# Fewer unread products in the prologue of a fused attention and MLP block, and one row tile moved from GpSimd to ScalarE

## The reference

```python
mod = (_silu(L0_c) @ L0_wmod).reshape(8, 6, 1, -1)
sa, ca, ga, sb, cb, gb = (mod[:, k] for k in range(6))
ga, gb = sign(ga) * max(|ga|, 0.25), sign(gb) * max(|gb|, 0.25)
h = _layernorm(x) * (1 + ca) + sa
scores = einsum('nsd,ntd->nst', h * w_lhs, h * w_rhs)
x = x + ga * einsum('nst,ntd->nsd', softmax(scores, axis=2), h)
h = _layernorm(x) * (1 + cb) + sb
x = x + gb * (relu(h @ W1 + b1) @ W2 + b2)
```

## Time and profile before

| | us |
|---|---|
| median of 3 runs | 678.64 |
| lowest and highest of them | 678.5, 679.3 |
| the profiled execution | 679.18 |
| its span in the trace | 677.4 |
| busy in it: TensorE | 672.5 |
| VectorE | 545.9 |
| ScalarE | 500.2 |
| GpSimd | 295.2 |

### The profile page before, as it was taken

The page is one execution under the profiler, slowest core; times in us unless marked ns, Lnnn a source line. Parts: engine busy times, 40 slices in busy tenths (PEclk is TensorE's granted clock), DMA queues, the critical chain, the costliest instruction groups (busy, mean ns, idle before and its releaser), DMA issues.

```text
span 677.4 us, 13532 instructions
## 1 busy us (share of the span) xinstructions
PE 672.5 (99%) x4551; PEld 620.4 (92%) x4551; DVE 545.9 (81%) x1139; ACT 500.2 (74%) x749; POOL 295.2 (44%) x311
## 2 busy tenths in 40 slices
PE   9999999999999999999999999999999999999998
PEld 8688889998999999999999989999899999999897
DVE  4798889887899879998799887988789987778321
ACT  2376787976889777895878949888688976747563
POOL 3551365225353345442645235542535334615544
PEclk9999999999999999999999999999999999999999
DMA  8131664237632377124671256513763246311210
GB/s 295 55 81 62 194 188 148 72 97 237 194 96 74 123 238 231 48 89 149 202 210 62 93 186 195 145 62 124 216 195 84 75 146 197 97 41 65 85 48 31
DMA packets 72897, 88.57 MB, mean 131 GB/s; under 512 B 6880, under 2 KB 64800, under 8 KB 72864
## 3 DMA queue, kind: packets, MB, share of 16 engines
q1 hardware_dynamic: 72864, 88.15, 41.6%
HBM read 51.66 MB, written 36.47 MB: 130 GB/s over the span
## 4 chain that ended last, share of the span: by engine, by line
PE 99%; DVE 0%; DMA 0%; issue 0%; SPq 0%
PE col L662 9%; PE col L661 9%; PE col L660 9%; PE acc L582 8%; PE acc L583 8%; PE acc L588 8%; PE score L766 8%; PE score L762 8%; PE score L763 8%; PE score L650 4%; PE score L651 4%; PE score L649 4%; PE score L755 4%; PE score L623 2%; PE score L551 1%; PE score L727 1%
## 5 line engine op out<-in xcount | busy, mean ns | idle before, releaser
L1249 POOL TENSOR_TENSOR hid_lo<-hid,hid_hi 128x512 fp32r<-128x512 f32 x127 | 175.9, 1387 | 258.3 <-ACT hid_hi L791 257.6
L787 ACT ACTIVATE hid<-col,b1T 128x512 f32<-128x512 f32 x128 | 87.1, 681 | 72.6 <-PE col L662 67.8
L582 PE MATMUL acc<-W2hi,hid_hi 128*128 128x256 f32 x480 | 118.0, 280 | 0.0
L583 PE MATMUL acc<-W2lo,hid_hi 128*128 128x256 f32 x480 | 116.6, 277 | 0.0
L762 PE MATMUL score<-V,Phi 128*128 128x258 f32 x448 | 108.7, 281 | 0.0
L763 PE MATMUL score<-V,Phi 128*128 128x256 f32 x448 | 108.5, 281 | 0.0
L662 PE MATMUL col<-h2hi,W1lo 128*128 128x512 f32 x256 | 101.0, 395 | 0.0
L660 PE MATMUL col<-h2hi,W1hi 128*128 128x512 f32 x256 | 100.7, 393 | 0.0
L661 PE MATMUL col<-h2lo,W1hi 128*128 128x512 f32 x256 | 100.7, 393 | 0.0
L791 ACT ACTIVATE hid_hi<-hid 128x512 fp32r<-128x512 f32 x128 | 81.0, 633 | 23.2 <-PE acc L588 15.6
L582 PEld LDWEIGHTS acc<-W2hi,hid_hi 128*128 128x128 f32 x480 | 90.3, 188 | 1.4
(11 more groups left out here) (168 smaller groups left out, 1476.5 us busy)
## 6 DMA issues: line engine op xcount, KB each, us to landing
block_rows<-blocks SPq DMA_DIRECT2D x29, 512.0 KB, 2.8
blocks<-block_rows SPq DMA_DIRECT2D x116, 128.0 KB, 2.9
x_cur<-x SPq DMA_DIRECT2D x16, 512.0 KB, 3.9
ln_t<-x SPq DMA_DIRECT2D x14, 512.0 KB, 4.8
score_blocks<-stage SPq DMA_DIRECT2D x14, 512.0 KB, 2.9
S<-score_blocks SPq DMA_DIRECT2D x56, 128.0 KB, 3.0
S<-quarter_blocks SPq DMA_DIRECT2D x56, 96.0 KB, 2.6
out<-x_mlp SPq DMA_DIRECT2D x8, 512.0 KB, 5.3
```

The source lines that it names most:

```text
L582: nc.tensor.matmul(o, hi, W2hi[:, it, :], start=(it == 0 and (apart or t % 2 == 0)), stop=False, skip_group_check=True)
L583: nc.tensor.matmul(o, hi, W2lo[:, it, :], start=False, stop=False, skip_group_check=True)
L787: nc.scalar.activation(hid[:, n % 2, :], col[n % 2][:], ACT.Relu, bias=b1T[:, n % FT:n % FT + 1]).then_inc(col_read, 1)
L1249: G.tensor_tensor(hid_lo[:, n % RING, :], hid[:, n % 2, :], hid_hi[:, n % RING, :].bitcast(F32), ALU.subtract).then_inc(hid_lo_done, 1)
```

## The change

- keep_busy runs 12 times at the start of MA.0 instead of 20.
- MF.1 and MF.0 have no unread products behind their pairs of products any more. The MA.0 step keeps its own.
- The fourth row tile of the second half is normalised on ScalarE, in a new step N0.1 between T0.0 and T0.1, which waits until rs and nb of that half are there. GpSimd's N0.1 keeps one row tile; its N0.0 keeps two.

```diff
     "act": """
-        MA.0+ T0.0+ T0.1+
+        MA.0+ T0.0+ N0.1+ T0.1+
     """,
...
                     elif kind == "MA":
                         pe.wait_ge(pool_const, 2)
-                        keep_busy(20)
+                        keep_busy(12)
...
                     elif kind == "MF":
                         pe.wait_ge(wmod_b_in, 16)
-                        last = modulation_by_feature((4, 3, 2, 5)[n], mod_b_ps[:, n * DK * NB:(n + 1) * DK * NB], 1 if ph is PH["before"] else 0)
+                        last = modulation_by_feature((4, 3, 2, 5)[n], mod_b_ps[:, n * DK * NB:(n + 1) * DK * NB], 0)
...
+                    elif kind == "N0":
+                        act.wait_ge(ln1_rstd, 2)
+                        nc.scalar.activation(V_first[:, T - 1, 0:D], x_cur[:, T - 1, :], ACT.Identity, scale=rs1[:, T - 1:T], bias=nb1[:, T - 1:T]).then_inc(v_first[1], 1)
...
                     elif kind == "N0":
                         pool.wait_ge(ln1_rstd, n + 1)
-                        for i in range(n * HT + 2, (n + 1) * HT):
+                        for i in range(n * HT + 2, (n + 1) * HT - n):
                             G.tensor_scalar(V_first[:, i, 0:D], x_cur[:, i, :], nm1[:, i:i + 1], rs1[:, i:i + 1], ALU.add, ALU.mult).then_inc(v_first[n], 1)
```

## The result

Twenty runs of the changed kernel have a median of 679.82 us (677.82 to 684.18), twenty of the kernel before 679.06 us (678.50 to 679.81). The means are 680.59 and 679.12 us. The ratio is 1.0023, with a 95% interval of 1.0012 to 1.0033: slower by 0.2%, where I had forecast 677.5 us.

A forecast was written before the change was run, and what follows sets the result against it. TensorE's queue, busy 99% of the span, was taken as the bound. T0.1 coming 1.25 us earlier took the profiled 679.18 to 677.9 us; the offset to the median led to 677.5 us, range 676.9 to 679.7.

The forecast's parts named there:

- third rival: TensorE falls to 1.2 GHz ahead of T0.1, or doesn't rise; T0.1 and SA take 2.6 us more, 680.1 us; chance 0.23.
- the eight: Leading products removed ahead of MA: 16 fast records, 1.7 us; MA starts near 6.77 us, 1.5 us earlier.
- its landing, 6.5 us: First two parts of wmod, issued at 1.84 us, land 4.7 us later, ahead of siluT at 6.71 us.
- nb (12.79 us) as the floor: GpSimd's chain stays and ends at 12.79 us; VectorE starts its two tiles at 12.83 us, not at 14.12.
- The four products between MF.1 and MF.0: Each removed product is 0.22 us, together 0.9 us; MF.1 and MF.0 shrink from 2.7 to 1.8 us.
- the sum: Prologue steps up to T0.1 added up: T0.1 1.12 to 1.37 us earlier than 14.97 us, taken as 1.25 us.
- T0.1 was put at 13.6 to 13.85 us: T0.1 starts between 13.60 and 13.85 us, released by VectorE, after TensorE stands idle some 0.75 us.
- The wait for the second part of wmod: Ahead of MF.1, this transfer lands at 11.1 us, giving TensorE a new wait of 0.3 to 0.4 us.
- ScalarE's tile: Row tile moved from GpSimd, 0.52 to 0.78 us, ending between 13.4 and 13.65 us, hidden behind VectorE.
- absorbed the shift: Behind T0.1 nothing was found to absorb the 1.25 us, so it reaches the end; nothing added for it.
- two ways to get to the median: From profiled 677.9 us: constant 0.54 us offset gives 677.4; if runs differ in clock rise, near 677.9; 677.5 taken.

The follow-up runs named there:

- e4: Kernel before with only the lead cut from 20 to 12 unread products; median 679.07 us, ratio 1.0017, clock fell in 6 of 12 runs.
- e8: Kernel before with its 20 leading products split, 12 ahead of the waits for siluT and wmod_a and 8 behind; median 680.05 us, ratio 1.0014.
- e6: Changed kernel with the load of wmod_a issued ahead of that of cT; median 681.22 us, ratio 1.0026, clock fell in 11 of 12.
- f3: Single profiled execution of the changed kernel with MF's four unread products back; 679.57 us, clock at 0.50 from 9.7 to 13.15 us.
- f4: Single profiled execution of the changed kernel itself; 682.50 us, mean clock 0.992, clock low from 9.5 to 19.8 us.
- f1: Single profiled execution of the changed kernel itself; 679.71 us, clock held up to T0.1, then slow from 14.8 us.
- e9: Changed kernel with a lead of 16 and MF's unread products back; median 678.32 us, ratio 0.9989, no fall in 11 runs.
- e5: Changed kernel with a lead of 16 unread products instead of 12; median 678.32 us, ratio 0.9991, clock fell in 2 of 11.
- e2: Changed kernel with one unread product again behind each pair of MF.1 and MF.0; median 679.94 us, ratio 1.003, clock fell in 9 of 12.
- e3: Kernel before with only the row tile moved to ScalarE; median 678.74 us, ratio 0.9996, no fall in 11 runs.
- e11: Changed kernel with a lead of 18 and MF's unread products back; median 678.62 us, ratio 0.9996, no fall in 11 runs.
- e1: Changed kernel with the 20 leading unread products back; median 679.37 us, ratio 1.0003, clock fell in 2 of 11.
- e7: Changed kernel with two unread products behind each pair in MA instead of one; median 680.70 us, ratio 1.0034, clock fell in 9 of 12.
- e10: Kernel before with eight of its 20 leading products moved into MA, three behind each pair; median 680.19 us, ratio 1.0036, fell in 3 of 12.
- f2: Single profiled execution of the changed kernel itself; 681.30 us, the clock falls at 8.2 us.

## Why the prediction was wrong

**What failed.** My third rival happened, and I gave it 0.23. It came in 16 of 20 runs. The step that failed is the sentence "Against it: the idle time is short, and products are issued all along". Neither protected the clock. e4 loses it in 6 of 12 runs with all the products between the modulation's parts in place and nothing cut but eight products of the lead. The same eight, put behind a pause of 1.0 us (e8), hold it in 11 of 11. So the pause alone does not do it, and MA's issuing all along did not stand in for the dense products. Whether a short lead would lose the clock without any pause was not tested, since e6 missed its aim; in f3 a pause of 0.3 us went with a fall.

I had the numbers to see that more was at stake. By my own reading the clock rises near 6.5 us and the twelve products end at 6.6 us. Before, 1.7 us of dense products at the full clock stood between the rise and the thin MA; after, none. I counted the eight only as 1.7 us to be gained.

In f4 the engine is busy all the time from 8 to 20 us, and the granted clock is 0.50 from 9.5 to 19.8 us. The Trainium skill, "TensorE: Matmul & The Clock Gate", Part 1, says that activity releases a throttle which is the default. The falls agree with it only if that activity is something else than the busy time which the profile shows.

**The price of the rival** was mis-sized too. I had T0.1 and SA double once, for 2.6 us on top of 677.5. The profiles of the changed kernel show falls at 8.2, 9.5, 10.3 and 14.8 us, which last 6.8, 10.2, 3.4 and 3.4 us. By the table of the result the first step costs 679.77 - 677.96 = 1.8 us, the next group lies 3.4 us, the last 5.9 us above full clock. So the commonest case was cheaper than my 2.6 us and the rarer ones dearer; that the median of 679.82 us lies near my 680.1 is in part luck. MA, T0.0 and MF, which I had left out, double like the rest.

**wmod_a.** I read its landing, 6.5 us, from one execution and took it as fixed. In all sixteen later profiles with its place in the queue unchanged it landed 5.1 to 5.7 us after its issue, so at 6.9 to 7.5 us. Before, a lead up to 8.29 us hid that. MA came at 7.1 to 7.7 us, not at 6.77. This was not free. In f1 the chain that leads to T0.1 runs back through VectorE's tiles, the R_first, T0.0 and MA to the landing of wmod_a at 7.02 us. VectorE's tiles started 0.28 us behind nb, and that is an estimate of what it cost.

**What VectorE's tiles wait for.** I had nb (12.79 us) as the floor and the R_first ending just ahead of it, at 12.7 us. In f1 the order is the other way round: nb is there at 12.67 us, the R_first end at 13.03 us because MA was late, and the tiles start at 12.95 us. So T0.1 hung on TensorE's own earlier steps, not on GpSimd. The profiles show almost the same distance from MA's first record to T0.1's where the clock held between them and MA is the same: 6.68 us before and in e9, where MF has its products, 6.71 in f1 and 6.51 in e5, where it has none. The four products between MF.1 and MF.0 thus cost 0.2 us at most while they were there, since VectorE needs about that time for the R_first and its tiles: the runs that held took 677.96 us without them against 678.13 with them (e2), and at a lead of 16 678.27 without (e5) against 678.32 with (e9). My own numbers said so: 6.77 + 6.68 = 13.45 us is earlier than the 13.60 I let T0.1 start at. Nearly all of the gain is MA's earlier start.

**What was right.** At full clock the sum held. T0.1 was put at 13.6 to 13.85 us, released by VectorE after an idle stretch of 0.75 us; in f1 its first record is at 13.86 us, after 0.73 us. That it fits so well is in part luck, as MA and the R_first were 0.3 to 0.4 us later than in the sum and nb 0.1 us earlier. The wait for the second part of wmod, 0.35 us in the sum, did not come up in f1, as T0.0 was late as well. ScalarE's tile, priced at 0.52 to 0.78 us, took 0.59 us and hid behind VectorE in f1 (it ends at 13.67 us, VectorE's at 13.80). Nothing behind T0.1 absorbed the shift: at full clock the changed kernel takes 677.96 us, 1.0 to 1.2 us under before. Of the two ways to get to the median, I chose the wrong one. The alternative I had named, 677.9 us, is where these runs are; they spread over 0.17 us, while before spreads over 1.3 us. That fits a kernel whose 20 leading products end sooner or later with the clock's rise against one that waits for a transfer, but no experiment tested this by itself, and the landing of wmod_a, on which T0.1 hangs in f1, varied by 0.6 us from profile to profile.

**What stays open.** How much dense work is enough, and how much its place counts beside its amount. A lead of 16 or more held the clock in all 33 runs that kept MF's products (e3, e9, e11) and in 18 of 22 of those that did not (e1, e5). So the four products between MF's pairs probably matter as well, in a second place: both profiled falls with such a lead begin at 14.4 and 15.9 us, in or behind the wait that follows the bare MF.

What makes one execution of a kernel fall and the next one hold is open too. One candidate is the moment of the first rise. By the traces' lists of clock changes it came at 4.57 to 6.85 us in the seven profiled executions with a lead of 12 straight ahead of MA that fell, and at 6.92 to 7.27 us in the three that held (e4, e7, e10). These are ten executions of six kernels, and nothing was done to move the rise.

A profile of the changed kernel with the clock held to the end was not obtained, and none of its slowest group either: a mean of 0.990 over 682 us is an estimated 2 x 0.010 x 682 = 14 us at 0.50, more than the 10.2 us of f4.

## What to carry to other kernels

Products that nothing reads may be holding the clock for work that comes much later: price their removal by what dense work is left up to the next long products, not by whether TensorE stays busy. Before that, ask whether they are in the way at all: those between MF's pairs were not, as another engine set the pace there. Take them away one place at a time, and compare the mean clocks of some ten or more runs; one profile shows one outcome of several, and the first three runs of the changed kernel (679.46, 677.98, 683.72 us) could be read in any way. Here, keeping 16 in the lead and all of the others (e9) gave 0.1%, without a fall in eleven runs.

## What the runs showed of the hardware

- Weight loads and products of 8 columns slow down with the granted clock like the wide ones: at 0.50 the sixteen records of MF took 3.3 us, at 1.00 1.70 us, and the cycle of two modulation products and one unread product took 1.28 us (9.46 to 10.74 us in f2) against 0.67.
- The granted clock stands at 1.00 in the profile's stretches before the first rise, though the records there have the spacing of the low level, 0.21 us. The first rise is read from the spacing of the weight loads, and came at about 4.6 us (f1), 5.7 (e6), 6.4 (before) and 7.6 (e5) in different executions of the same opening.
- One program took 677.8 to 684.2 us, in groups that its mean clock (1.000 to 0.989) tells apart. Every slow stretch that was profiled up to 20 us lasted 3.4, 6.8 or 10.2 us.
